# Differential attention plus soft mixture of experts: last stage reads back stored softmax weights and turns them on TensorE

## The reference, cut to what matters

```python
logits = (jnp.einsum('tzd,ed->tze', x, phi_w) + phi_b).reshape(t, z, n, p)
D = jax.nn.softmax(logits, axis=3)     # dispatch: over the 32 slots of an expert
C = jax.nn.softmax(logits, axis=2)     # combine: over the 64 experts of a slot
X_tilde = jnp.einsum('tznp,tzd->npd', D, x)
...
Y_tilde = jnp.einsum('npd,ndH->npH', X_tilde, expert_w) + expert_b[:, None, :]
Y = jnp.einsum('tznp,npH->tzH', C, Y_tilde)
```

## Time and profile before

| what | before |
|---|---|
| median of 3 runs | 1433.09 us (1432.4 to 1435.12) |
| the profiled execution, own time | 1433.77 us |
| its span | 1432.0 us |
| setup, main, experts, combine (from the timeline) | 33.7, 1180.0, 28.7, 189.6 us |
| TensorE matmuls busy | 1352.1 us, 94% of the span |
| ScalarE, GpSimd, VectorE busy | 1146.4, 1130.4, 1091.4 us |
| DMA | 59.14 MB moved, mean 41 GB/s |

### The profile page before, as it was taken

One profiled execution on the slowest core, in us unless ns is written; L12 is line 12 of the kernel. 1 busy time (PEld: TensorE's weight loads), 2 busy tenths in 40 slices (PEclk: granted clock), 3 DMA queues, 4 the chain that ended last, 5 costly groups with the idle time before them and its releaser, 6 DMA issues. The chain is left out here.

```text
span 1432.0 us, 28403 instructions
## 1 busy us (share of the span) xinstructions
PE 1352.1 (94%) x9298; PEld 1034.8 (72%) x9425; DVE 1091.4 (76%) x1915; ACT 1146.4 (80%) x3354; POOL 1130.4 (79%) x878
## 2 busy tenths in 40 slices
PE   3899999999999999999999999999999997699998
PEld 2677777777777777777777777777777774588886
DVE  6677887788778887888788878887888776655554
ACT  4778888888888888878887888788878885699997
POOL 2468888888888788878887888888888888299997
PEclk8999999999999999999999999999999998799999
DMA  5110111111111111111111111111111100600101
GB/s 167 47 35 35 36 45 38 37 36 47 38 36 36 47 38 36 36 47 38 36 36 47 38 36 36 47 38 36 36 36 36 37 7 15 150 15 15 31 15 31
DMA packets 64419, 59.14 MB, mean 41 GB/s; under 512 B 17536, under 2 KB 45200, under 8 KB 64144
## 3 DMA queue, kind: packets, MB, share of 16 engines
q1 hardware_dynamic: 60608, 55.86, 12.2%
q10 hardware_dynamic: 3664, 1.44, 0.4%
HBM read 15.34 MB, written 2.10 MB: 12 GB/s over the span
## 5 line engine op out<-in xcount | busy, mean ns | idle before, releaser
L668 ACT ACTIVATE e<-ps_s,neg_max 128x256 f32<-128x256 f32 (+1 forms) x1024 | 414.3, 430 | 135.4 <-DVE neg_max L740 135.4
L740 DVE TENSOR_REDUCE neg_max<-ps_s 128x2 f32<-128x512 f32 (+1 forms) x384 | 241.3, 684 | 138.6 <-PE ps_s L531 138.6
L880 POOL TENSOR_TENSOR disp<-logit,gmax 128x512 f32<-128x512 f32 x128 | 134.5, 1051 | 251.4 <-DVE gmax L783 251.4
L655 ACT ACTIVATE pT<-ps_t 128x512 f32<-128x512 f32 x384 | 238.1, 621 | 65.7 <-PE ps_t L506 64.9
L888 POOL TENSOR_TENSOR e<-e,inv 128x1024 f32<-128x1024 f32 x128 | 284.5, 2223 | 0.0
L506 PEld LDWEIGHTS ps_t<-ident,e 128*128 128x128 f32 x1536 | 186.1, 140 | 85.6 <-issue 65.5
L506 PE MATMUL ps_t<-ident,e 128*128 128x128 f32 x1536 | 229.9, 272 | 1.2 <-ACT pT L655 1.2
L668 ACT ACTIVATION_READ_ACCUMULATOR e<-ps_s,neg_max 128x1 f32 x1024 | 221.5, 216 | 0.0
L531 PE MATMUL ps_s<-qk 64*128 64x256 f32 (+1 forms) x2048 | 202.4, 337 | 18.5
L531 PEld LDWEIGHTS ps_s<-qk 64*128 64x128 f32 x2048 | 172.9, 186 | 44.5 <-issue 40.6
L1130 POOL TENSOR_TENSOR c_lo<-cT,c_hi 128x512 fp32r<-128x512 f32 x128 | 165.7, 1300 | 39.5 <-ACT cT L1173 29.2
(11 more groups left out here) (147 smaller groups left out, 3092.7 us busy)
## 6 DMA issues: line engine op xcount, KB each, us to landing
xs<-xT SPq DMA_DIRECT2D x128, 256.0 KB, 2.4
fx<-xT SPq DMA_DIRECT2D x64, 64.0 KB, 1.9
fxn<-xn SPq DMA_DIRECT2D x32, 64.0 KB, 1.9
xres<-in_L_attn_x SPq DMA_DIRECT2D x8, 256.0 KB, 3.2
out_dram<-res SPq DMA_DIRECT2D x8, 256.0 KB, 2.4
xn<-in_L_attn_x SPq DMA_DIRECT2D x2, 512.0 KB, 6.9
xn<-in_L_attn_x ACTq DMA_DIRECT2D x2, 512.0 KB, 7.8
bias<-in_L_ffn_phi_b SPq DMA_DIRECT2D x1, 1024.0 KB, 6.8
```

The lines of the kernel that those rows point to most:

```text
L655: nc.scalar.activation(pT[:, k, :], ps_t[:, (q + k) % 2, :], ACT.Copy).then_inc(t_out, 1)
L668: ins = nc.scalar.activation(dst, ps_s[:, k, i * width:(i + 1) * width], ACT.Exp, bias=neg_max[:, q, c:c + 1], accum_out=total[:, q, c:c + 1])
L740: nc.vector.tensor_reduce(neg_max[:, q, c:c + heads], ps_s[:, k, :].rearrange("p (h t) -> p h t", h=heads), AX.X, ALU.max, negate=True).th ...
L880: nc.gpsimd.tensor_tensor(by_expert(bank_of(disp, t, jj)), by_expert(bank_of(logit, t, jj)), gmax[:, jj, :].unsqueeze(2).to_broadcast([P, ...
```

## The change

In the main stage SyncE stores each bank of exponentials (128 partitions by 512, 256 KB) to a scratch tensor in DRAM after its exponential (`store_weights`, 128 stores). So that the bank stays intact, the sum over the banks runs in a buffer of its own, `c_run`, and the `logit` half is free again only when its store has landed (`c_stored`, waited for by `take_logits`). GpSimd's addition now waits until `slot_sum` of the tile before has read `c_run` (`c_sum`). `m_all` keeps two tiles instead of 32.

In the experts stage the logarithm and the two additions go; VectorE takes the reciprocal of the 1024 sums right after the clip, GpSimd makes one copy and ScalarE two. The transposes and copies that made `lseT` now make `c_invT`. SyncE issues the first three reloads (1 MB each) behind `eb`.

In the combine stage SyncE reloads the weights in 32 pieces of four tiles by 512 columns (three buffers, `c_back`); each step makes four transposes on TensorE instead of three matmuls, VectorE multiplies by `c_invT` on emptying PSUM, ScalarE makes one rounded copy, and the rounding rest is formed by GpSimd in three steps of four and by VectorE in the fourth (`low`). The transposed bias `phibT` and its load, transpose and copy in the setup stage go.

```diff
@@ setup_phase
-            sp.dma_start(phib_rows[:], env["phi_b"].rearrange("(t p) -> t p", p=P)).then_inc(loaded["phib"], 16)
...
-            pe.wait_ge(loaded["phib"], 16)
-            pe.transpose(ps_b[:, 0:NST], phib_rows[:], ident[0:NST, 0:NST]).then_inc(phib_done, 1)
@@ main_phase, sync
+            def store_weights(t, j):
+
+                if live(t, NTT):
+                    sp.wait_ge(c_exp, 4 * t + j + 1)
+                    sp.dma_start(c_dram[t, j], bank_of(logit, t, j)).then_inc(c_stored[t % 2][j], 16)
+
             def iteration(it, kk, g):
                 load_xs(2 * it + 2, 0, (2 * kk + 2) % NPAIR)
+                store_weights(*back(it, 0, 6))
+                store_weights(*back(it, 1, 6))
...
                 load_xs(2 * it + 3, 1, (2 * kk + 3) % NPAIR)
+                store_weights(*back(it, 2, 6))
+                store_weights(*back(it, 3, 6))
                 load_tile(it)
...
+            for n in range(4 * NTT - 6, 4 * NTT):
+                store_weights(n // 4, n % 4)
+            for r in range(2):
+                for j in range(4):
+                    sp.wait_ge(c_stored[r][j], 16 * (NTT // 2))
@@ main_phase, vector: take_logits and slot_sum
-                if j < 3:
-
-                    wait(dve, c_bank, 3 * (t - 2) + j + 1)
-                else:
-                    wait(dve, c_sum, t - 1)
+                if t >= 2:
+
+                    dve.wait_ge(c_bank, 3 * (t - 2) + max(j, 1))
+                    dve.wait_ge(c_stored[t % 2][j], 16 * (t // 2))
...
-                                            by_expert(bank_of(logit, t, 3)).rearrange("p e s -> p s e"), AX.X,
+                                            by_expert(c_run[:]).rearrange("p e s -> p s e"), AX.X,
@@ main_phase, gpsimd
-                    bank = bank_of(logit, t, jj)
-                    nc.gpsimd.tensor_tensor(bank, bank, bank_of(logit, t, jj - 1), ALU.add).then_inc(c_bank, 1)
+                    wait(pool, c_sum, t)
+                    so_far = bank_of(logit, t, 0) if jj == 1 else c_run[:]
+                    nc.gpsimd.tensor_tensor(c_run[:], so_far, bank_of(logit, t, jj), ALU.add).then_inc(c_bank, 1)
@@ experts_phase
+            for n in range(len(c_back)):
+                load_weights(sp, env, n)
             sp.wait_ge(ew_in, 16)
...
-            nc.scalar.activation(ln_c[:], c_all[:], ACT.Ln).then_inc(lnc_done, 1)
...
-            nc.gpsimd.tensor_tensor(lse[:, :, 0, :], by_tile, m_tiles, ALU.add).then_inc(lse_done, 1)
-            nc.gpsimd.tensor_tensor(lse[:, :, 1, :], by_tile, m_tiles, ALU.add).then_inc(lse_copies, 1)
+            pool.wait_ge(inv_done, 1)
+            nc.gpsimd.tensor_copy(c_inv[:, :, 1, :], c_inv[:, :, 0, :]).then_inc(inv_copies, 1)
...
             nc.vector.tensor_scalar(xt_acc[:], xt_acc[:], -33000.0, 65000.0, ALU.max, ALU.min).then_inc(clip_done, 1)
+            nc.vector.reciprocal(c_inv[:, :, 0, :], c_all[:].rearrange("p (t s) -> p t s", s=NP_)).then_inc(inv_done, 1)
@@ new
+def load_weights(eng, env, n):
+
+    p, j = divmod(n, 4)
+    q = n % len(env["c_back"])
+    eng.dma_start(env["c_back"][q][:], env["c_dram"][4 * p:4 * p + 4, j].rearrange("t p n -> p t n")
+                  ).then_inc(env["c_back_in"][q], 16)
@@ combine_phase, sync (exchange holds the loads of x and the stores of the result, as before)
+            for n in range(NB_, 4 * NPAIR + NB_):
+                if n < 4 * NPAIR:
+                    sp.wait_ge(ct_mm, 4 * (n - NB_ + 1))
+                    load_weights(sp, env, n)
+                if (n - NB_) % 4 == 2:
+                    exchange((n - NB_) // 4)
@@ combine_phase, tensor
-                product3(pe, ps_l[:, n % RL, :], phiT[0][:, w], phiT[1][:, w], xT[0][:, tok], xT[1][:, tok]
-                         ).then_inc(lt_mm, 1)
+                c, st = divmod(n, 4)
+                if st == 0:
+                    pe.wait_ge(c_back_in[c % NB_], 16 * (c // NB_ + 1))
+                wait(pe, ct_out, n - RL + 1)
+                for i in range(4):
+                    mm = pe.transpose(ps_c[:, n % RL, i * P:(i + 1) * P], c_back[c % NB_][:, i, st * P:(st + 1) * P],
+                                      ident[:])
+                mm.then_inc(ct_mm, 1)
@@ combine_phase, scalar
-                nc.scalar.activation(c_hi[:, n % R, :], lg[:, n % RL, :], ACT.Exp, bias=phibT[:, st:st + 1])
-                nc.scalar.activation(cT[:, n % R, :], lg[:, n % RL, :], ACT.Exp,
-                                     bias=phibT[:, st:st + 1]).then_inc(c_exp, 1)
+                nc.scalar.activation(c_hi[:, n % R, :], cT[:, n % R, :], ACT.Copy).then_inc(c_high, 1)
@@ combine_phase, vector
+            def low(n):
+                if n >= 0 and n % 4 == 3:
+                    dve.wait_ge(c_high, n + 1)
+                    wait(dve, y_mm, n - R + 1)
+                    nc.vector.tensor_tensor(c_lo[:, n % R, :], cT[:, n % R, :], f32(c_hi[:, n % R, :]),
+                                            ALU.subtract).then_inc(low_dve, 1)
...
-                nc.vector.tensor_tensor(lg[:, n % RL, :], ps_l[:, n % RL, :], lseT[:, p * PT:(p + 1) * PT],
-                                        ALU.subtract).then_inc(lg_out, 1)
+                nc.vector.tensor_tensor(cT[:, n % R, :], ps_c[:, n % RL, :], c_invT[:, p * PT:(p + 1) * PT],
+                                        ALU.mult).then_inc(ct_out, 1)
+                low(n - 1)
```

More of the change, by code:

```diff
@@ L409, in main_phase @@
                  dict(p0=0, p1=1, p2=0, p3=1, lg=0, xt=1))
+        c_stored = [[sem(f"c_stored{r}{j}") for j in range(4)] for r in range(2)]
         SB = (1, 2, 0)
@@ L430, in main_phase @@
         x_sb, xs, a_w, v_w, wo_w = env["xn"], env["xs"], env["a_w"], env["v_w"], env["wo_w"]
-        fx, bias = env["fx"], env["bias"]
+        fx, bias, c_dram = env["fx"], env["bias"], env["c_dram"]
         PER = NPAIR // 2
@@ L1114, in _, with exchange @@
         def _(sp):
-            for p in range(NPAIR + 1):
+            def exchange(p):
                 if p < NPAIR:
@@ L1126, in _ @@
         def _(pool):
-            for n in range(NST * NPAIR):
-                pool.wait_ge(c_exp, n + 1)
-                wait(pool, y_mm, n - R + 1)
-                nc.gpsimd.tensor_tensor(c_lo[:, n % R, :], cT[:, n % R, :], f32(c_hi[:, n % R, :]),
-                                        ALU.subtract).then_inc(c_low, 1)
+            for n in range(NC):
+                if n % 4 < 3:
+                    pool.wait_ge(c_high, n + 1)
+                    wait(pool, y_mm, n - R + 1)
+                    nc.gpsimd.tensor_tensor(c_lo[:, n % R, :], cT[:, n % R, :], f32(c_hi[:, n % R, :]),
+                                            ALU.subtract).then_inc(low_pool, 1)
         @block.tensor
@@ L1140, in untranspose, with turn @@
                 mm.then_inc(f_mm, 1)
-            def logits_t(n):
-                p, st = divmod(n, NST)
-                w, tok = slice(st * P, (st + 1) * P), slice(p * PT, (p + 1) * PT)
-                wait(pe, lg_out, n - RL + 1)
-                product3(pe, ps_l[:, n % RL, :], phiT[0][:, w], phiT[1][:, w], xT[0][:, tok], xT[1][:, tok]
-                         ).then_inc(lt_mm, 1)
+            def turn(n):
+                c, st = divmod(n, 4)
[6 more added lines that the diff above has]
+                mm.then_inc(ct_mm, 1)
             def mix(n):
                 p, st = divmod(n, NST)
-                pe.wait_ge(c_low, n + 1)
+                pe.wait_ge(c_high, n + 1)
+                if n % 4 < 3:
+                    pe.wait_ge(low_pool, 3 * (n // 4) + n % 4 + 1)
+                else:
+                    pe.wait_ge(low_dve, n // 4 + 1)
                 if st == 0:
@@ L1155, in mix @@
                          c_lo[:, n % R, :], start=(st == 0), stop=(st == NST - 1)).then_inc(y_mm, 1)
-            for n in range(NST * NPAIR + LAG):
-                if n < NST * NPAIR:
-                    logits_t(n)
+            for n in range(NC + LAG):
+                if n < NC:
+                    turn(n)
                 if n >= LAG:
@@ L1201, in _ @@
                     add_x(p - 1)
+            low(NC - 1)
             finish(NPAIR - 1)
@@ L1220, in shared_buffers @@
     env["neg_lam"] = sb("neg_lam", [P, 1])
+    env["xn"] = sb("xn", [P, NTT, D])
+    env["xT"] = [sb(f"xT{h}", [P, NT], F32R) for h in range(2)]
+    env["phiT"] = [sb(f"phiT{h}", [P, NS_], F32R) for h in range(2)]
 def build(nc, x, wq, wk, wv, wo, lq1, lk1, lq2, lk2, phi_w, phi_b, expert_w, expert_b, out):
@@ L1241, in build @@
         env["mask"] = sb("mask", [P, G, P], BF16)
[L1242 to L1245 removed]
         env["o_acc"] = sb("o_acc", [P, NT])
         env["xt_acc"] = sb("xt_acc", [P, NS_])
[L1248 removed]
+        env["m_all"] = sb("m_all", [P, 2 * NP_])
         env["c_all"] = sb("c_all", [P, NTT * NP_])
@@ L1254, in build @@
         env["y_t"] = [sb(f"y_t{h}", [P, NST, D], F32R) for h in range(2)]
-        env["lseT"] = sb("lseT", [P, NT])
+        env["c_invT"] = sb("c_invT", [P, NT])
```

(2 more changed lines are left out.)

77 lines of the change are left out of this document (33 added, 44 removed).

## The result

The changed kernel takes 1398.12 us (median of four runs, 1397.33 to 1399.31) against 1433.33 us for the kernel before, measured beside it on the same chip: a ratio of 0.9754, 95% interval 0.9737 to 0.977. The forecast was 1401.

A forecast was written before the change was run, and what follows sets the result against it. TensorE, busy 94% of the span, was taken as the bound: 1433.8 - 33.7 (combine steps) - 0.8 (its end) + 1.6 (main stage's end) + 1.0 (experts) = 1401.9, less 0.7 for the median, so 1401 us; own range 1396 to 1408, stated range 1394 to 1420.

The forecast's parts named there:

- The bound and the combine step: Combine stage: TensorE sets the pace; four transposes for three matmuls cut a step from 1.393 to 1.13 us, 33.7 us less.
- Start and end of the stage: Combine stage: start at the lower clock as before, last rest formed faster by VectorE; -0.8 us, between -1.4 and 0.
- The other engines: Combine stage: GpSimd 15.6, VectorE 16.4, ScalarE 10.1 us fit into TensorE's 18.5 us per group, VectorE with 11% to spare.
- The reload: Combine stage: weights reloaded at 255 GB/s, hidden by three buffers giving 9 us; cost 0, up to 3 us if late.
- The lower bound of 173 GB/s: Combine stage: slowest rate considered for the reload, taken from the broadcast of `eb`; a group would take 27.3 us.
- The main stage: Main stage: added stores hidden and TensorE's work unchanged, so 0, bounds -0.5 and +16 us; only its end pays.
- +1.6: Main stage's end: GpSimd's first addition of the last tile waits for VectorE's reduction of the tile before; 1.6 us later.
- The experts stage: Experts stage: a 6.5 us reciprocal delays the expert matmuls 3.5 us, 2.4 covered by the `eb` wait; +1, between 0 and +3.
- The first: Rival, combine stage: VectorE or GpSimd becomes the bound, giving back 9 to 22 us; 1410 to 1423 us, chance 13%.
- the third: Rival, combine stage: reload too slow, TensorE waits for `c_back`; 1471 us at 173 GB/s, chance 6%.
- The second: Rival, main stage: the stores delay operand loads, costing up to 16 us; 1402 to 1417 us, chance 11%.
- the fourth: Rival, combine stage: TensorE's clock falls because transposes do not hold it, a step takes 2.3 us; 1551 us, chance 2%.

The follow-up runs named there:

- three_matmuls: Changed kernel with three 512-column matmuls of other data in place of the four transposes in each combine step; 1428.7 us.
- after_again: The changed kernel itself, unedited, run again for comparison with the other runs of the chip; 1398.87 us, ratio 0.9754 to the kernel before.
- two_sums: Changed kernel with two running-sum buffers by tile parity, so GpSimd's first addition no longer waits for VectorE's reduction of the tile before; 1397.81 us.
- rest_all_gpsimd: Changed kernel with every rounding rest of the combine stage formed by GpSimd, none by VectorE; 1411.46 us.
- two_buffers: Changed kernel with two reload buffers in place of three; 1414.02 us.
- only_transposes: Changed kernel with six transposes in place of the three mixing matmuls, so TensorE runs only transposes in the combine stage; 1392.3 us.
- experts_shorter: Changed kernel with two running sums, expert bias loaded before the expert weights, these in four quarters, and reciprocals taken per tile in the main stage; 1394.16 us.
- copy_for_reciprocal: Changed kernel with VectorE's reciprocal of the 1024 sums replaced by a copy of the same shape; 1397.42 us.

## Why the prediction was right, step by step

**The bound and the combine step: right.** 1.13 us was read from a place in the main stage that runs the same mix; the stage shows 1.127. 128 x (1.393 - 1.127) = 34.0 us, predicted 33.7. Of this, 3.8 us belong to what the three matmuls that went multiplied, by three_matmuls. The sum needed no word on that, since it took the step before from the very matmuls that were to go.

**Start and end of the stage: right in size, not in its reason.** Outside steps and turn-backs the stage had 189.6 - 128 x 1.393 - 8 x 0.44 = 7.8 us before and has 154.8 - 128 x 1.127 - 3.5 = 7.0; the forecast was 0.8 less. But "the start runs at the lower clock as before" failed in the profiled execution, where TensorE started at the full clock (1.00; 0.70 in after_again), and this bought little because the first rests came late.

**The other engines: they fit, with more room than said.** GpSimd was as forecast: 12 x 1.299 = 15.6 us per group. VectorE's `low` was taken at 0.995 us and measured 0.755, so VectorE has 110 - 85.2 = 24.8 of 110 us left, 23% and not 11. The row taken, from the main stage, was too far; the near row, 0.687, was the better one.

**The reload: right.** 260 GB/s against 255 forecast, landing in 5.9 us within the 9 that three buffers give, no wait on `c_back` in the stage. The lower bound of 173 GB/s had to do with the broadcast, not with the reload.

**The main stage: the step that failed.** The sum had 0 for the stage and +1.6 for its end; measured -0.5 in all. That is -2.7 us up to VectorE's last `take_logits` (1156.6 to 1153.8 us from the first matmul) and +2.2 behind it (23.4 to 25.6). The +1.6 is there (1.6 on average over nine profiles). The "0" was -2.7: in the eleven profiles with the change the last `take_logits` starts at 1152.7 to 1154.8, in the two without it at 1156.6 and 1158.2. TensorE's waits for the logits' PSUM bank, by the waits view of the main stage before and after, show most of it:

```profile
PE ps_tu L76 <- DVE logit L776: 9.4, 11, 1.3
```

```profile
PE ps_tu L76 <- DVE logit L783: 7.6, 11, 1.3
```

That is 1.8 us: seven of the eleven, one in every fourth tile, fell from 0.85 to 1.21 us each to 0.65. Why `take_logits` was late there shows in VectorE's timeline, before and after:

```profile
467.31 1.04 DVE L820 TENSOR_REDUCE c_all<-logit 128x32 f32<-128x512 f32 x1
468.46 0.69 DVE L776 TENSOR_TENSOR logit<-ps_tu,bias 128x512 f32<-128x512 f32 x1
```

```profile
467.44 1.03 DVE L827 TENSOR_REDUCE c_all<-c_run 128x32 f32<-128x512 f32 x1
468.40 0.67 DVE L783 TENSOR_TENSOR logit<-ps_tu,bias 128x512 f32<-128x512 f32 x1
```

Before, `take_logits` of the fourth bank waited (`c_sum`) for the slot sum that VectorE itself had just run, since that sum read the bank to be filled; it started 0.11 us after the sum's end. Now the sum reads `c_run`, the wait is gone, and `take_logits` starts 0.07 us before the sum's recorded end. Over the 30 tiles the median from start to start is 0.99 us in place of 1.19. This is a wait that the change loosens; the prediction bounded that at -0.5, since it "freed nothing I could see". A look at the waits view of before would have shown 9.4 us in eleven waits for `take_logits`, the instruction that carries it. No run puts the old wait alone back, and some 0.9 us more, outside these waits, have no row.

**The experts stage: right in mechanism, 0.9 us too high here, by luck of the clock.** The reciprocal took 6.55 us (6.5 forecast), `bn_stats` started at 1221.51 (1221.5), its run took 3.13 us (3.2), the wait for the root fell from 1.04 to 0.28. The delay reached the sixteen transposes ahead of the expert matmuls as forecast: they started 3.4 us later (1230.33 to 1233.76). But they took 2.14 us in place of 3.20, at granted clock 0.89 in place of 0.58. So the expert matmuls started 2.4 us later, not 3.5, their first quarter ended at about 1235.82 + 3.70 / 4 = 1236.7 and not 1237.9, and the wait for `eb`, over at 1237.15, covered the whole: +0.1 against +1.0. In two_sums and three_matmuls, with the transposes at granted clocks of 0.59 and 0.60, the stage took 29.9 us, 1.2 more than before, as the prediction had it.

The Trainium skill, "VectorE: DVE Perf Modes", section "Walkthrough: the 8-slice pipeline in each mode", gives Reciprocal a repeat count of 8, from which the prediction estimated 8.5 us; the row of 6.55 us decides, 6.4 ns per column, as the slope of the two short ones said. The prediction's floor of 1.2 us misread its row: the clip runs 2048 columns in 1.23 us, so 1024 at its rate take 0.6.

**The rivals.** The first is real without the split (rest_all_gpsimd: 1411.5, in its range of 1410 to 1423), the third without the third buffer (two_buffers). The second and the fourth do not exist here. The Trainium skill, "TensorE: Matmul & The Clock Gate", section "Part 4: PE-mode transpose", holds that the full clock doesn't engage for transposes; only_transposes, 110 us of them at clock 1.00, disagrees.

**The total.** By stages: setup +0.7, main -0.5, experts +0.1, combine -34.8, together -34.5; the forecast was 0, +1.6, +1.0 and -34.5, together -31.9. The 2.6 us between them are most of the 2.9 us by which the median lies below 1401, and nearly all of them lie in the main stage's "0". These terms are read from one profile each; in kernels whose code is the same there, single stages differ by 1 to 2.5 us.

## What to carry to other kernels

Where one engine has no gaps, read the price of the new mix of its instructions from a place in the same trace that already runs that mix, and the price of the old from the very instructions that go; the rest of the work is to show that each other engine and the transfer fits into the shorter step, which here hung on one rest in four and on a third buffer. An operation put in front of a wait for a DMA costs nothing until it is longer than the wait, and taking it away gains little either (0 to 1.4 us here): move both, as experts_shorter did. Before a wait is called free to loosen, sum up who waits behind it, by the waits view of that stage, and look at what the instruction that they wait for had itself waited for.

## What was not expected of the hardware

- f32 transposes alone keep TensorE at the granted clock of 1.00: 0.11 us each for 110 us.
- Matmuls of the same shape and type came 0.232 or 0.227 us apart at the same granted clock, by what the stage multiplies; exchanging the operands of three matmuls in six shortened all six.
- An instruction of VectorE that waited for the one just before it on VectorE started 0.11 us after that one's end; without the wait it started 0.07 us before it.
- Stores of 256 KB beside the reload landed in 6.1 us, where they took 2.4 before; no engine's wait in the stage is for them.
- At the end of the main stage the same matmuls run at either clock from one kernel to the next: two of L562, after 0.88 us of waiting for VectorE in both, took 2.04 us at granted clock 0.50 in the changed kernel (from 1203.57) and 1.10 us at 1.00 in copy_for_reciprocal (from 1202.20). From the last `take_logits` to the clip this made 25.6 or 24.7 us. The whole main stage varied by 2.5 us between kernels whose code there is the same, so single profiles of such kernels can't be compared below that.
